# A quantised feed-forward whose block scales are worked out for two tiles at once

## The reference

```
scale = maximum(max(|xb|) / 6, 1e-12);  xn = xb / scale
q = GRID[searchsorted(MID, |xn|)] * sign(xn) * scale
```

## Time and profile before

| what | value |
|---|---|
| time, median of 3 runs | 1329.28 us (1324.35 to 1331.13) |
| time of the profiled execution | 1323.85 us |
| its span in the profile | 1322.0 us |
| TensorE busy | 1169.1 us, 88% |
| VectorE busy | 1049.7 us, 79% |
| ScalarE busy | 732.5 us, 55% |
| GpSimd busy | 576.1 us, 44% |
| mean granted TensorE clock | 0.985 |

### The profile page before, as it was taken

How to read it: one execution, slowest core, us unless ns; L and a number is a source line. 1 busy time by engine, 2 the same in 40 slices (tenths; PEclk the granted TensorE clock), 3 DMA queues, 4 the chain that set the end, 5 groups by cost and what they waited for, 6 DMA issues and landing times.

```text
span 1322.0 us, 25381 instructions
## 1 busy us (share of the span) xinstructions
PE 1169.1 (88%) x7664; PEld 741.8 (56%) x7664; DVE 1049.7 (79%) x3443; ACT 732.5 (55%) x1475; POOL 576.1 (44%) x530
## 2 busy tenths in 40 slices
PE   0459999999998779998998999999999999999997
PEld 0226555555555456675666667566665555555554
DVE  4769999999999856546654764664799999999996
ACT  3556666666665435444543444465566666766653
POOL 1244445444544434443443444345344554454441
PEclk9879999999999989999999999999999999999998
DMA  9524434443443546664655566546355445444555
GB/s 317 116 54 81 88 74 86 78 89 72 88 78 71 106 81 101 120 115 94 108 102 105 97 116 119 98 79 125 63 97 105 102 100 107 103 105 98 109 105 115
DMA packets 462749, 134.46 MB, mean 102 GB/s; under 512 B 441296, under 2 KB 461904, under 8 KB 462672
## 3 DMA queue, kind: packets, MB, share of 16 engines
q1 hardware_dynamic: 454928, 125.62, 49.0%
q10 hardware_dynamic: 7744, 7.86, 1.9%
HBM read 11.34 MB, written 8.39 MB: 15 GB/s over the span
## 4 chain that ended last, share of the span: by engine, by line
DVE 31%; issue 26%; PE 25%; ACT 7%; POOL 7%; DMA 1%; SPq 1%; DVEq 1%; ACTq 1%; POOLq 0%
PE ps L1449 11%; PE ps L1437 8%; DVE arena L914 5%; DVE arena L974 4%; POOL arena L522 3%; DVE arena L918 3%; POOL arena L511 2%; DVE arena L1080 2%; DVE arena L903 2%; PE ps L1422 2%; ACT arena L645 2%; DVE arena L863 2%; PE ps L1402 2%; ACT arena L684 2%; PE ps L1415 2%
## 5 line engine op out<-in xcount | busy, mean ns | idle before, releaser
L1402 PE MATMUL ps<-wguT,arena 128*128 128x512 f16 (+1 forms) x2304 | 480.0, 363 | 28.7 <-DVE m_sb L1320 14.7
L1402 PEld LDWEIGHTS ps<-wguT,arena 128*128 128x128 f16 x2304 | 225.9, 98 | 250.6 <-issue 30.5
L522 POOL TENSOR_TENSOR arena<-arena 128x704 f32<-128x704 f32 x128 | 192.1, 1501 | 342.0 <-DVE arena L927 334.6
L1369 PE MATMUL ps<-wdT,arena 128*128 128x256 f16 x2176 | 264.2, 276 | 59.3 <-DMA arena<-arena 55.9
L1369 PEld LDWEIGHTS ps<-wdT,arena 128*128 128x128 f16 x2176 | 206.5, 99 | 124.5 <-issue 74.3
L549 POOL TENSOR_TENSOR arena<-arena 128x128 f16<-128x128 f32 (+7 forms) x64 | 143.8, 2247 | 236.6 <-ACT arena L745 197.7
L691 ACT ACTIVATE arena<-arena 128x704 int16<-128x704 f32 x128 | 100.9, 788 | 211.9 <-POOL arena L522 211.9
L1449 PE MATMUL ps<-arena 128*128 128x256 f16 x1632 | 188.9, 273 | 9.0 <-DVE x_sb L1096 8.9
L1437 PE MATMUL ps<-arena 128*128 128x512 f16 (+3 forms) x960 | 188.7, 349 | 3.5 <-ACT arena L745 3.5
L754 ACT ACTIVATE arena<-ps,arena,cst 128x128 f16<-128x128 f32 (+7 forms) x64 | 80.4, 1257 | 194.7 <-DVE arena L1085 190.7
L1449 PEld LDWEIGHTS ps<-arena 128*128 128x128 f16 x1632 | 158.3, 98 | 36.1 <-DVE x_sb L1096 7.2
(11 more groups left out here) (121 smaller groups left out, 1429.8 us busy)
## 6 DMA issues: line engine op xcount, KB each, us to landing
out_dram<-x_sb SPq DMA_DIRECT2D x32, 256.0 KB, 2.7
x_sb<-in_L_attn_x_dram ACTq DMA_DIRECT2D x3, 2048.0 KB, 17.8
arena<-arena SPq DMA_TRANSPOSE x384, 3.5
arena<-arena SPq DMA_DIRECT2D x8, 256.0 KB, 2.9
arena<-arena SPq DMA_DIRECT2D x4, 512.0 KB, 3.4
x_sb<-in_L_attn_x_dram ACTq DMA_DIRECT2D x1, 1536.0 KB, 7.4
arena<-in_L_ffn_w_down_dram SPq DMA_DIRECT2D x1, 704.0 KB, 8.4
arena<-in_L_ffn_w_gate_dram SPq DMA_DIRECT2D x1, 640.0 KB, 4.5
```

What stands on the lines that cost most here:

```text
L522: g.tensor_tensor(hy[u].rearrange("p (j b) -> p b j", j=BL), h[u].rearrange("p (b j) -> p b j", j=BL), hri[u].unsqueeze(2).to_broadcast([P ...
L1369: i = nc.tensor.matmul(ps_dn[w % 2], hT[w][:, c * P:(c + 1) * P], wdT[:, k, :], start=(s == 0), stop=(s == len(DOWN_STEPS) - 1))
L1402: i = nc.tensor.matmul(psf[:, 1536 * u + lo:1536 * u + hi], xv[:, u, xl, kt, :], wguT[:, wl, lo // P:hi // P, kt, :], start=(s == 0), stop ...
```

## The change

- The scale chain of h runs once for a pair: `ham`, `hs`, `hri`, `hsp`, `hsd` and the two float16 parts are single buffers of 88, and `dve_h_s` to `dve_h_sl` are issued once on 88 scales. Maximum, power, inverse and factor have two columns. `dve_h_sp` becomes a `tensor_tensor` with the inverse broadcast.
- Codes come in the same step as their scales: `dve_h_g` and `dve_h_q` of both tiles of pair gp stand in `dve_pair(gp)`. `dve_h` and `dve_h_amax` in that step are those of pair gp + 1.
- x's operations stand between those of the h chain. `dve_x_sd` moves from the end of the step before to just after `dve_h_max`.
- GpSimd does both `pool_h_y` of a pair one behind the other, then `pool_x_rstd(gp + 3)`, then `pool_x_y(gp + 3)`.
- ScalarE and SyncE follow: `act_h_n` and `act_h_c` of both tiles in the pair's own step, `sp_h_T` of both tiles together behind `sp_x_T`.
- The operations for the attention's first keys (`z`) at the end of the first phase move to places inside the pairs, and so do the two late attention additions.

```diff
-        ham = [carve(HB) for _ in range(2)]
-        hs = [carve(HB) for _ in range(2)]
...
+        ham, hs, hri, hsp, hsd = (carve(2 * HB) for _ in range(5))
+        hsp2 = carve(4 * HB, f16)
+        hmx, hpw, hin = (carve(2) for _ in range(3))
...
-        def pool_pair(gp, odd, x3=True, x4=True, z1=False):
-            pool_h_y(2 * gp, 0)
-            if z1:
-                pool_z_lo(1)
-            pool_h_y(2 * gp + 1, 1)
+        def pool_pair(gp, odd, x3=True):
+            for u in range(2):
+                pool_h_y(gp, u)
             if x3:
+                pool_x_rstd(gp + 3, 1 - odd)
                 pool_x_y(gp + 3)
-            if x4:
-                pool_x_rstd(gp + 4, odd)
...
+        def act_pair(gp, p, odd, x2=True, x3=True, x4=True, end=False, z=None):
+            if x2:
+                act_x_n(gp + 2)
+            if not end:
+                act_silu(2 * gp + 2, 0)
             for u in range(2):
...
+                act_h_n(2 * gp + u, u)
+                act_h_c(2 * gp + u, u)
+            if x3:
+                act_x_z(gp + 3, p + 3)
+            if x4:
+                act_x_mean(gp + 4, p + 4, odd)
...
+            if not end:
+                act_silu(2 * gp + 3, 1)
...
+            if x4:
+                act_x_squares(gp + 4, p + 4, odd)
...
+        def dve_h_sp(gp):
+            V.wait_ge(h_in, gp + 1)
+            V.tensor_tensor(of_two(hsp), of_two(hs), hin.unsqueeze(2).to_broadcast([P, 2, HB]), ALU.mult
+                            ).then_inc(h_sp, 1)
...
+        def dve_pair(gp, qd, p, odd, start=None, x2=True, x3=True, end=False, add=None, z=None):
+
+            more, down = not end, start is None or start >= 2
+            dve_h_s(gp)
+            dve_h_rin(gp)
+            dve_h_max(gp)
+            if x2:
+                dve_x_sd(gp + 2)
+            dve_h_pow(gp)
+            if x2:
+                dve_x_c(gp + 2)
+                dve_x_sh(gp + 2)
+            dve_h_inv(gp)
+            if down:
+                dve_res(gp - 2, odd, 0, p * 2 - 4)
+            if x2:
+                dve_x_g(gp + 2)
+                dve_x_sl(gp + 2)
+            dve_h_sp(gp)
+            if down:
+                dve_res(gp - 2, odd, 1, p * 2 - 3)
+            if x2:
+                dve_x_q(gp + 2, 0, (qd + odd, 1 - odd))
+            dve_h_sd(gp)
+            if x2:
+                dve_x_q(gp + 2, 1)
+            dve_h_sh(gp)
+            dve_h_fc(gp, odd)
...
+            dve_h_sl(gp)
+            if more:
...
+                dve_h(2 * gp + 2, 0)
+            dve_h_g(2 * gp, 0)
+            if more:
+                dve_h_amax(2 * gp + 2, 0)
+            dve_h_q(gp, 0, quad(qd, 2 * odd - 2))
+            dve_h_g(2 * gp + 1, 1)
+            dve_h_q(gp, 1, quad(qd, 2 * odd - 1))
+            if x3:
+                dve_x_amax(gp + 3)
+                dve_x_s(gp + 3)
+                dve_x_rin(gp + 3)
...
+            if more:
...
+                dve_h(2 * gp + 3, 1)
+                dve_h_amax(2 * gp + 3, 1)
```

More of the change, by code:

```diff
@@ L155, in macaron_block_kernel @@
         hq = [carve(2 * F, f16) for _ in range(2)]
-        ham = [carve(HB) for _ in range(2)]
-        hs = [carve(HB) for _ in range(2)]
[L158 to L166, removed]
+        ham, hs, hri, hsp, hsd = (carve(2 * HB) for _ in range(5))
+        hsp2 = carve(4 * HB, f16)
+        hsh, hsl = hsp2[:, 0:2 * HB], hsp2[:, 2 * HB:4 * HB]
+        hmx, hpw, hin = (carve(2) for _ in range(3))
+        hfc = [carve(2) for _ in range(2)]
         assert at[0] <= pT_late
@@ L362, in sp_h_T, with sp_pair @@
             nc.sync.dma_start_transpose(hT[w].rearrange("p (c r) -> p c r", r=P), hq[w % 2]).then_inc(h_T[w], 16)
-        def sp_pair(gp, odd, first=False, x2=True, free=None):
-            if not first:
-                sp_h_T(gp * 2 - 1, (2 * odd - 1) % 4)
+        def sp_pair(gp, odd, x2=True, free=None):
             if x2:
@@ L458, in _ @@
             for k in range(NP):
[L459 to L465, removed]
+                sp_pair(k, k % 2, x2=(k < NP - 2))
+                if k == NP - 3:
+                    sp_z_T(0)
+            sp_z_T(1)
             sp_keys_z(0)
@@ L484, in _ @@
                 if k < NP:
-                    sp_pair(NP + k, k % 2, first=(k == 0), x2=(k < NP - 2), free=NT if k == 0 else None)
-                if k == NP:
-                    sp_h_T(2 * NT - 1, 3)
+                    sp_pair(NP + k, k % 2, x2=(k < NP - 2), free=NT if k == 0 else None)
                 if k >= 2:
@@ L559, in pool_slot @@
             for q in range(4):
-                if last and s == X_SLOT[q]:
+                if last and q < 3 and s == X_SLOT[q]:
                     pool_x_rstd(NP + q, q % 2)
@@ L602, in _ @@
             pool_x_y(2)
-            pool_x_rstd(3, 1)
             pool.wait_ge(m_amax, 1)
@@ L623, in _ @@
                 for k in range(NP - 4, NP):
[L624 to L629, removed]
+                    pool_pair(first + k, k % 2, x3=(k < NP - 3))
+                    if not first:
+                        if k == NP - 4:
+                            pool_z_rstd(0)
+                        if k == NP - 3:
+                            pool_z_lo(0)
+                        if k == NP - 2:
+                            pool_z_rstd(1)
+                        if k == NP - 1:
+                            pool_z_lo(1)
         def act_hold_wait(k):
@@ L697, in act_h_c @@
             nc.scalar.activation(hc[u], hn[u], ACT.Copy, scale=0.25 * CODE, bias=0.125 * CODE).then_inc(h_c, 1)
-        def act_pair(gp, p, odd, start=None, x2=True, x3=True, x4=True, z1=False):
-            for u in range(2):
[L701 to L717, removed]
+        def act_pair(gp, p, odd, x2=True, x3=True, x4=True, end=False, z=None):
[3 more added lines that the diff above has]
+                act_silu(2 * gp + 2, 0)
+            for u in range(2):
+                act_h_n(2 * gp + u, u)
[4 more added lines that the diff above has]
+                act_x_mean(gp + 4, p + 4, odd)
+            if z == 0:
+                act_z_hi(z)
+            if not end:
+                act_silu(2 * gp + 3, 1)
+            if z == 1:
+                act_z_hi(z)
+                act_load_table(ACT.Exp)
+            if x4:
+                act_x_squares(gp + 4, p + 4, odd)
         def act_z_hi(g):
@@ L837, in _ @@
                     act.wait_ge(p_lo, NT)
-                act_pair(first, 0, 0, start=0)
-                act_pair(first + 1, 1, 1, start=1)
+                for u in range(2):
+                    act_silu(2 * first + u, u)
+                act_pair(first, 0, 0)
+                act_pair(first + 1, 1, 1)
                 if not first:
@@ L846, in _ @@
                 for k in range(NP - 4, NP):
[L847 to L853, removed]
+                    act_pair(first + k, k, k % 2, x2=(k < NP - 2), x3=(k < NP - 3), x4=(k < NP - 4), end=(k == NP - 1),
+                             z=None if first else {NP - 3: 0, NP - 2: 1}.get(k))
                 if not first:
@@ L917, in dve_h_amax @@
             V.wait_ge(h_h, n + 1)
-            V.tensor_reduce(ham[u], h[u].rearrange("p (b j) -> p b j", j=BL), axis=AX.X, op=ALU.max,
+            V.tensor_reduce(ham[:, u * HB:(u + 1) * HB], h[u].rearrange("p (b j) -> p b j", j=BL), axis=AX.X, op=ALU.max,
                             apply_absolute_value=True).then_inc(h_amax, 1)
-        def dve_h_s(n, u):
-            V.wait_ge(h_amax, n + 1)
-            V.tensor_scalar(hs[u], ham[u], SIXTH, SCALE_MIN, ALU.mult, ALU.max).then_inc(h_s, 1)
@@ L925, in dve_h_rin @@
[L925 to L957, removed]
@@ L959, in dve_h_sl, with of_two, dve_h_s, dve_h_rin @@
-        def dve_h_sl(n, u):
-            V.wait_ge(h_sh, n + 1)
-            V.tensor_tensor(hsl[u], hsp[u], hsh[u], ALU.subtract).then_inc(h_sl, 1)
+        def of_two(v):
+            return v.rearrange("p (u b) -> p u b", u=2)
+        def dve_h_s(gp):
+            V.wait_ge(h_amax, 2 * gp + 2)
+            V.tensor_scalar(hs, ham, SIXTH, SCALE_MIN, ALU.mult, ALU.max).then_inc(h_s, 1)
+        def dve_h_rin(gp):
+            V.wait_ge(h_s, gp + 1)
+            V.reciprocal(hri, hs).then_inc(h_rin, 1)
@@ new lines, in dve_h_max, with dve_h_pow, dve_h_inv @@
+        def dve_h_max(gp):
+            V.wait_ge(h_s, gp + 1)
+            V.tensor_reduce(hmx, of_two(hs), axis=AX.X, op=ALU.max).then_inc(h_mx, 1)
+        def dve_h_pow(gp):
+            V.wait_ge(h_mx, gp + 1)
+            V.tensor_scalar(hpw.bitcast(i32), hmx.bitcast(i32), EXP_BITS, None, ALU.bitwise_and).then_inc(h_pw, 1)
+        def dve_h_inv(gp):
+            V.wait_ge(h_pw, gp + 1)
+            V.tensor_scalar(hin.bitcast(i32), hpw.bitcast(i32), -1, H_INV_BITS, ALU.mult, ALU.add).then_inc(h_in, 1)
@@ L966, in dve_h_g, with dve_h_q @@
             V.tensor_scalar(v, v, ROUND_CODE, ROUND_CODE, ALU.add, ALU.subtract).then_inc(h_g, 1)
[L968 to L972, removed]
+        def dve_h_q(gp, u, landed):
+            V.wait_ge(h_g, gp * 2 + (u + 1))
+            if u == 0:
```

(72 more changed lines are left out.)

42 lines of the change are left out of this document (34 added, 8 removed).

## The result

The changed kernel takes 1420.05 us, the median of four runs (1417.83 to 1421.08), against 1329.92 before (1324.35 to 1331.13): a ratio of 1.070 (95% interval 1.066 to 1.073). It is slower by 90 us. The profiled execution has a span of 1416.0 us, 94.0 more than before.

What follows compares the result with a forecast made beforehand. VectorE was taken to bound the kernel at 12.05 us a pair; 11.07 + 2.4 + 0.15 gave 13.6. 52 steady pairs add 81 us, 12 others 12, making 1417, and 5.4 for the median gives 1420; forecast range 1385 to 1450.

Steps and rivals of the forecast that it cites:

- the 5.4 added for the median: Final sum: the median of the runs lies 5.4 us above the profiled execution, taking 1417 to a predicted 1420.
- What bounds the kernel: Feed-forward pairs: VectorE sets the 12.05 us period; TensorE needs 10.84 and has 1.2 to spare.
- What the merge gives: VectorE's scale chain: saves 1.28 us a pair, dependent neighbours cost 0.61, so 11.07 without GpSimd.
- the loop's wait: VectorE's 0.31 us wait at the end of a two-pair loop body; half, 0.15, was added to each pair.
- the 0.11 from max to pow: Merged chain on VectorE: pow would wait for max to end, costing 0.11 us, part of the 0.61.
- What GpSimd takes back: Behind the reciprocal: x_c and x_sh held by both pool_h_y, 1.18 + 1.35, taken as 2.4 us a pair.
- Who is served first: When VectorE and GpSimd ask for the port at once: the trace showed no case, so left open.
- Rival 2: VectorE keeps the port while it has work for it: loss 1.4, period 12.6, about 1360 us; chance 0.14.
- rival 1: GpSimd does not hold VectorE and only the saving remains: period 11.2, about 1275 us; chance 0.14.
- rival 4: TensorE's lower clock adds 0.3 to a loss of 2.9: period 14.4, about 1460 us; chance with beyond 0.06.
- Charging nothing: TensorE's slower products after its idle gap, 0.8 to 1.8 us, counted as free; 0.3 a pair in the upper bound.
- Ends and attention: Outside the 52 steady pairs: 12 other pairs add 12 us; prologue and ends nothing, within 3 us either way.

Runs made afterwards that it cites:

- e1: Changed kernel, but GpSimd multiplies only 2 of the 16 columns of each block in pool_h_y, leaving most of that product out; 1281.81 us, 0.967 of the kernel before.
- e3: Changed kernel with both dve_res, then dve_h and dve_h_amax, moved up behind dve_h_max, and four buffers of h; 1313.79 us, 0.991 of the kernel before.
- e5: e3 with both dve_h_g ahead of both dve_h_q and dve_x_amax between the two dve_h_q; 1287.43 us, 0.970 of the kernel before.
- e4: Kernel before, without the merge, with dve_x_sh and dve_x_c moved up behind dve_res, where pool_h_y runs; 1375.59 us, 1.037 of the kernel before.
- e2: Changed kernel with both dve_res moved up to just behind dve_h_max, beside GpSimd's pool_h_y; 1388.8 us, 1.047 of the kernel before.

## Why the prediction was right

The forecast of 1420 us and the median of 1420.05 agree more closely than the working deserves. The sum gave 1417 for the profiled execution, which took 1417.83; the 5.4 added for the median would make 1422, and the median lies 2.2 above that execution. The terms one by one:

- *What bounds the kernel.* VectorE, with TensorE close behind. e1, e3 and e5 changed only what stands on or beside VectorE's path and moved the pair between 11.2 and 13.7 us.
- *What the merge gives.* 11.07 us was worked out for VectorE without GpSimd, 11.2 with half the loop's wait. e1 gives 11.42 less 0.33 of holding, 11.09. The lengths on 88 scales came out as read from the prologue, the reciprocal 0.70 (0.69), the start of the chain 0.92 behind the last maxima (0.93). Two terms, 0.26 together, came to nothing, and others were 0.13 too small, which is luck. The 0.15 for the loop's wait: no idle time of 0.3 before the chain is left in the changed kernel or in e1. And the 0.11 from max to pow: `dve_x_sd` stands between the two, and in the timeline above they start 0.10 and 0.12 apart, as without a wait.
- *What GpSimd takes back.* Predicted 1.18 + 1.35, taken as 2.4; measured 1.30 + 1.18 = 2.48. The pair was predicted at 13.6 and is 13.65.
- *Who is served first.* This was open, though the sum took one of the ways. In the steady pairs of the changed kernel it comes out as the sum had it: `pool_h_y`, one VectorE operation (x_c), the second `pool_h_y`, then x_sh. Rival 2, in which VectorE keeps the port, falls: its pair was 12.6. Mostly the earlier start wins. In 52 pairs x_c starts 0.03 to 0.04 behind a `pool_h_y` and is held; in 7, at the ends of the phases, it starts 0.02 to 0.03 ahead of one and lasts 0.3, and that `pool_h_y` lasts 1.62 to 1.66. The second `pool_h_y` starts 0.2 ahead of x_sh.
- *The port does not bite* (rival 1, 1275 us) falls with the two lines at 1.59 and 1.36, and with e4. Its number was nearly that of e1, 1282, where most of GpSimd's share is taken out: the saving was real, the price was larger.
- *TensorE at the lower clock* (rival 4). The gap is there, 2.55 us, and the down product behind it takes 3.23 instead of 2.02, the gate and up product 4.25 instead of 3.73, at the granted clocks given above. By starts that is 7.10 us for the two (223.13 to 230.23) instead of 5.42, 1.68 more, and the next gap is only 1.10, both as predicted. Charging nothing was nearly right: only the `dve_h` at 230.43 waits for the slow product, and the 24 of 50 steady pairs with such a stretch take 13.72 us against 13.59 for the others, 3 us in all.
- *Ends and attention.* 52 steady pairs of +1.59 are 83 us (predicted 81). The other pairs of the phases add 14 (predicted 12), and attention, prologue and tail give 3 back (predicted nothing, within 3).

The Trainium skill (SBUF — State Buffer, "Who interferes with whom") says that the second of the two engines blocks until the first is through. The traces agree: a 32-element operation was held for 1.05 us in e4, and with `pool_h_y` cut short in e1 the holds of 1.30 and 1.18 shrank to 0.18 and 0.15.

What I mis-sized was in e2: I counted the moved work as pure gain. The first hold shrank by 0.67 and not by 0.78, and the second grew by 0.14, because the operation before it is shorter.

## What to carry to other kernels

Before GpSimd work on SBUF operands is moved or bunched, list which VectorE instructions will stand beside it: here reductions, operations with one operand in PSUM and a tensor_scalar on one column ran at full speed, and SBUF-to-SBUF tensor_scalar on more columns, two-input and 16-bit operations stood still until GpSimd was done. A saving in instruction count is worth having only once that list is clean: the same merge was 7% slower in one order and 3% faster in another, which needed two more buffers of h. When an engine's instruction is much longer than its least, look at what the other engine ran in just that time before blaming the instruction.

## What the runs showed of the hardware that was not expected

- In the steady pairs of the changed kernel one VectorE operation runs between two GpSimd operations that follow each other (1.58 and 1.36 us on two operations in a row); in e2 it is `dve_x_sd` and the short `dve_h_pow` behind it (0.81 and 0.17, then 1.60). It is no fixed alternation. In 7 pairs of the changed kernel a held `dve_h_pow` and then x_c go ahead of the second `pool_h_y`. In the kernel before, `dve_h_q` (214.17) went behind the held `dve_h_sp` although `pool_x_rstd` had started at 214.16. And late in e2's second phase `dve_h_pow` waits through both `pool_h_y`:

```profile
1361.60 2.87 POOL L510 TENSOR_TENSOR arena<-arena 128x704 f32<-128x704 f32 x2 [8.80 <-DVE arena L918]
1362.32 2.18 DVE L926 TENSOR_SCALAR arena<-arena 128x2 int32<-128x2 int32 x1
```

  In e3 the same operation, at the same distance from the same `pool_h_y`, waits for the first only and lasts 0.80. What decides such a case stays open.
- A second column makes the difference for `dve_h_pow`. On one column, in the kernel before, it never lasts over 0.154 us, though more than 120 of its 128 stand beside a `pool_h_y`. On two, in the changed kernel, 11 of its 64 start behind a `pool_h_y` and last 1.43 to 1.47; in the steady pairs it starts just ahead (219.66 against 219.70) and escapes:

```profile
L935 DVE TENSOR_SCALAR arena<-arena x128: 134/142/154, 62.4 to 1306.9; 128x1 int32<-128x1 int32 x128
```
```profile
L926 DVE TENSOR_SCALAR arena<-arena x64: 168/170/1469, 64.9 to 1399.5; 128x2 int32<-128x2 int32 x64
```

- The held time shows as a longer VectorE instruction, not as idle time: ahead of L875 the page lists one wait of 4.9 us in the whole span, and none for GpSimd, though L875 and L867 together spent some 138 us held (64 of each, less 0.28 and 0.18 for each).
